# The output projection of a window-attention block: one float32 product becomes three float16 products, with their split on GpSimd

## The reference, cut to what matters

```python
f = _ln(f, g1, b1); f = jnp.roll(f, (-SS, -SS), axis=(1, 2)); win = _window_partition(f)
qkv = win @ w_qkv + b_qkv
attn = softmax(q k^T * scale + mask)
out = einsum('bhij,bhjd->bihd', attn, v).reshape(-1, L, C)
out = out @ w_proj + b_proj                  # the projection that is changed
f = residual + roll_back(window_reverse(out))
m = gelu(_ln(f, g2, b2) @ w_fc1 + b_fc1) @ w_fc2 + b_fc2
return f + m
```

## Time and profile before

| | |
|---|---|
| median of 3 runs | 2864.15 us (2864.08 to 2870.08) |
| the profiled execution | 2863.74 us, its span 2861.9 us |
| busy share of the span | PE 95%, PEld 78%, DVE 85%, ACT 74%, POOL 64% |
| granted TensorE clock | 0.995 of full speed |
| instructions | PE 55491, DVE 6634, ACT 3464, POOL 2344 |

### The profile page before, as it was taken

One profiled execution on the slowest core, in us unless ns is written; L12 is line 12 of the kernel. 1 busy time (PEld: TensorE's weight loads), 2 busy tenths in 40 slices (PEclk: granted clock), 3 DMA queues, 4 the chain that ended last, 5 costly groups with the idle time before them and its releaser, 6 DMA issues.

```text
span 2861.9 us, 138054 instructions
## 1 busy us (share of the span) xinstructions
PE 2724.4 (95%) x55491; PEld 2241.3 (78%) x55491; DVE 2427.8 (85%) x6634; ACT 2113.9 (74%) x3464; POOL 1844.0 (64%) x2344
## 2 busy tenths in 40 slices
PE   4999999999999999999999999999999999999996
PEld 2788787888878878878878888887887887878885
DVE  7888888888888888888888888888888888888884
ACT  2677777777777777777777777777777777777774
POOL 4566666666666666666666666666666666666665
PEclk9999999999999999999999999999999999999998
DMA  3454544545545445454454554544545445455441
GB/s 84 125 131 127 133 128 129 132 124 133 132 124 132 129 128 132 125 133 128 129 134 124 131 132 126 131 129 127 133 126 132 126 130 134 124 131 132 127 118 29
DMA packets 414852, 358.88 MB, mean 125 GB/s; under 512 B 63646, under 2 KB 414176, under 8 KB 414204
## 3 DMA queue, kind: packets, MB, share of 16 engines
q1 hardware_dynamic: 414220, 350.04, 46.7%
HBM read 193.29 MB, written 154.14 MB: 121 GB/s over the span
## 4 chain that ended last, share of the span: by engine, by line
PE 69%; DVE 18%; issue 7%; ACT 5%; POOL 1%; SPq 0%; DMA 0%; POOLq 0%; DVEq 0%
PE psum L530 11%; PE psum L438 9%; PE psum L512 8%; DVE nmax L856 7%; PE psum L570 7%; DVE yr L920 6%; PE psum L618 6%; PE psum L494 6%; ACT probs L719 4%; PE psum L652 4%; PE psum L555 3%; PE psum L448 3%; PE psum L608 3%; PE psum L456 3%; PE psum L658 3%
## 5 line engine op out<-in xcount | busy, mean ns | idle before, releaser
L719 ACT ACTIVATE probs<-psum 113x784 f32<-113x784 f32 x768 | 631.2, 822 | 314.7 <-PE psum L512 311.6
L856 DVE TENSOR_REDUCE nmax<-psum 113x16 f32<-113x784 f32 x768 | 743.1, 968 | 70.3 <-PE psum L494 70.1
L530 PE MATMUL psum<-vbd,probs 128*49 128x18 f32 x24576 | 643.1, 197 | 7.4 <-issue 6.6
L530 PEld LDWEIGHTS psum<-vbd,probs 128*49 128x49 f32 x24576 | 632.5, 126 | 10.7 <-issue 10.5
L399 POOL TENSOR_SCALAR ve<-mv 112x7 f32<-112x7 f32 (+1 forms) x264 | 65.4, 248 | 876.5 <-PE psum L570 638.1
L512 PE MATMUL psum<-qbd,kst 128*49 128x196 f16 x6144 | 405.1, 250 | 36.6 <-issue 16.8
L494 PE MATMUL psum<-kbd,qst 128*49 128x196 f16 x6144 | 402.4, 250 | 27.9 <-DVE nmax L856 25.0
L406 POOL TENSOR_TENSOR rs<-ve,half 112x7 f32<-112x7 f32 (+1 forms) x264 | 394.1, 1493 | 0.0
L411 POOL TENSOR_TENSOR xn<-xn,rs 112x672 f32<-112x672 f32 (+1 forms) x264 | 342.2, 1296 | 73.9 <-POOL rs L406 73.9
L880 DVE BATCH_NORM_STATS2 st<-tok 112x6 f32<-112x96 f32 x1824 | 318.2, 245 | 58.9 <-ACT tok L726 44.8
L392 POOL TENSOR_TENSOR hidl<-hid,hidh 128x588 f16<-128x588 f32 x256 | 333.6, 1303 | 46.2 <-POOL hidh L389 46.2
(11 more groups left out here) (102 smaller groups left out, 6166.7 us busy)
## 6 DMA issues: line engine op xcount, KB each, us to landing
stack_pages<-nat SPq DMA_DIRECT2D x256, 294.0 KB, 3.1
kst<-stack_pages SPq DMA_DIRECT2D x256, 220.5 KB
qbd<-stack_pages SPq DMA_DIRECT2D x1024, 55.1 KB
stack_pages<-nat SPq DMA_DIRECT2D x256, 147.0 KB, 2.0
xr<-in_x_dram SPq DMA_DIRECT2D x224, 147.0 KB, 2.7
out_dram<-yr SPq DMA_DIRECT2D x224, 147.0 KB, 2.1
qst<-stack_pages SPq DMA_DIRECT2D x256, 73.5 KB
kbd<-stack_pages SPq DMA_DIRECT2D x1024, 18.4 KB
```

The lines of the kernel that those rows point to most:

```text
L530: last = nc.tensor.matmul(dst[:, :, h, :], probs[:, b.c % 2, h // 4, p, h % 4 * L:(h % 4 + 1) * L], vbd[:, b.c % 4, p * NH + h, :, :], sta ...
L719: nc.scalar.activation(probs[0:PR, b.c % 2, u, :, :].rearrange("j (g q) k -> j g (q k)", g=2), wide_bank()[0:PR, LEFT:LEFT + 8 * SPAN].rea ...
L856: nc.vector.tensor_reduce(dst, psum[0:PR, A:A + 2, 0:2 * CH].rearrange("i g (q h j) -> i g q h j", q=2, j=L), axis=AX.X, op=ALU.max, negat ...
```

## The change

The projection becomes three float16 products like the others. Its weights are multiplied by 64 and split once (`split_wp`, DVE); its bias becomes a 97th row of the weights, against a row of ones in `oTh`. POOL gets a new job in every step, `split_out`: a rounding of `oT` to `oTh` and a subtraction into `oTl`, 96 x 392 each. It stands in POOL's queue behind `split_hidden` and ahead of `normalise`. The projection waits for the second of the two (`o_low`) instead of for ACT's copy, and `residual` scales by 1/64.

The order changes too. PE: in even steps `contract` goes ahead of `project`, which is then last; in odd steps `scores` 0 goes ahead of `values`, and `out_transposes` goes from behind the expands to right behind `turn`. ACT: in odd steps `out_by_channel` goes ahead of the two gelus, and a gelu of one element stands right behind the third exp. DVE: in odd steps `residual` goes behind `back_low` and `queries_keys_low`. At the start, one of the 15 constant loads (the bias row) is issued only after DVE has filled the padding rows.

```diff
+            const(wp[C:C + 1, :], bproj.rearrange("(a c) -> a c", a=1))
...
+            def split_out(b):
+                pool.wait_ge(o_in, b.count(2, 2))
+                alone(pool)
+                wait(pool, proj_made, b.count(1))
+                alone(pool)
+                nc.gpsimd.tensor_copy(oTh[0:C, :], oT[:, :]).then_inc(o_high, 1)
+                pool.wait_ge(o_high, b.count(1, 1))
+                alone(pool)
+                nc.gpsimd.tensor_tensor(oTl[0:C, :], oT[:, :], oTh[0:C, :], ALU.subtract).then_inc(o_low, 1)
...
                             split_hidden(t.step(offset))
+                if has(t.step(WEIGH)):
+                    split_out(t.step(WEIGH))
...
-                pe.wait_ge(o_in, b.count(2, 2))
+                pe.wait_ge(o_low, b.count(1, 1))
...
-                nc.tensor.matmul(psum[0:C, V_BANK, 0:TOK], wp[:, :], oT[:, :], start=True, stop=True).then_inc(proj_made, 1)
+                for n, (weights, rows) in enumerate(((wph, oTh), (wph, oTl), (wpl, oTh))):
+                    last = nc.tensor.matmul(psum[0:C, V_BANK, 0:TOK], weights[:, :], rows[:, :], start=n == 0, stop=n == 2)
+                last.then_inc(proj_made, 1)
...
                     shifted(t, 0)
+                    scores(t, 0)
                     values(t)
-                    scores(t, 0)
...
                     turn(t)
+                    out_transposes(t)
                     expand(t, 0)
...
                     max_transpose(t)
-                    out_transposes(t)
                     back(t)
...
                     queries_keys(t)
+                    contract(t)
                     project(t)
-                    contract(t)
...
+            nc.vector.memset(spare[:, :], 0.0).then_inc(filled, 1)
             dve.wait_ge(filled, 1)
+            nc.vector.memset(oTh[C:C + 1, :], 1.0)
...
+            def split_wp():
+                nc.vector.tensor_scalar(wp[:, :], wp[:, :], GAIN, None, ALU.mult).then_inc(wp_split, 1)
+                dve.wait_ge(wp_split, 1)
+                nc.vector.tensor_copy(wph[:, :], wp[:, :]).then_inc(wp_split, 1)
+                dve.wait_ge(wp_split, 2)
+                nc.vector.tensor_tensor(wpl[:, :], wp[:, :], wph[:, :], ALU.subtract).then_inc(wp_split, 1)
...
+            def gelu_table(t):
+                nc.scalar.activation(spare[0:1, 1:2], spare[0:1, 0:1], ACT.Gelu)
...
                     run(PROB, exps, 2)
+                    run(HIDDEN[0], gelu_table)
+                    run(WEIGH, out_by_channel)
                     run(HIDDEN[0], gelu, 0)
                     run(HIDDEN[1], gelu, 1)
-                    run(WEIGH, out_by_channel)
...
                 before = t.step(-1)
-                run(before, WEIGH, residual)
                 if odd(t):
                     if turns(before.step(BACK)):
                         back_low(before)
                     run(before, QK, queries_keys_low)
+                run(before, WEIGH, residual)
+                if odd(t):
                     run(t, STORE[0], result, 0)
```

More of the change, by code:

```diff
@@ L119, in build @@
         wp, w2 = sb("wp", [FULL, C]), sb("w2", [FULL, 3, C])
-        vec = sb("vec", [C, 6])
-        G1, B1, BP, G2, B2, BF = range(6)
+        vec = sb("vec", [C, 5])
+        G1, B1, G2, B2, BF = range(5)
         xr = sb("xr", [C, 4, WS, SIDE])
@@ L139, in build @@
         on = sb("on", [PR, 2, 2, C])
-        oT = sb("oT", [FULL, TOK])
+        oT = sb("oT", [C, TOK])
+        spare = sb("spare", [1, 2])
+        oTh, oTl = sb("oTh", [FULL, TOK], F16), sb("oTl", [FULL, TOK], F16)
+        wph, wpl = sb("wph", [FULL, C], F16), sb("wpl", [FULL, C], F16)
         hid = sb("hid", [FULL, 2, 3, PART])
@@ L182, in build @@
         ot_made, o_in, proj_made, f_made = sem("ot_made"), sem("o_in"), sem("proj_made"), sem("f_made")
-        w2_split = sem("w2_split")
+        w2_split, wp_split = sem("w2_split"), sem("wp_split")
+        o_high, o_low = sem("o_high"), sem("o_low")
         hid_high, hid_low, w2_wide, y_scaled = sem("hid_high"), sem("hid_low"), sem("w2_wide"), sem("y_scaled")
@@ L264, in _ @@
             const(brow1[C:C + 1, :], bfc1.rearrange("(a c) -> a c", a=1))
-            for n, v in ((G1, g1), (B1, b1), (BP, bproj), (G2, g2), (B2, b2), (BF, bfc2)):
+            for n, v in ((G1, g1), (B1, b1), (G2, g2), (B2, b2), (BF, bfc2)):
                 column(n, v)
             sp.wait_ge(filled, 1)
+            const(wp[C:C + 1, :], bproj.rearrange("(a c) -> a c", a=1))
             sp.dma_start(xfh[C:C + 1, :, :, :].rearrange("a n k t -> a (n k) t"), rows_d[0, 4:5, 0:8, :]).then_inc(rows_one, 16)
@@ L614, in project @@
                     return
-                pe.wait_ge(o_in, b.count(2, 2))
+                pe.wait_ge(o_low, b.count(1, 1))
                 if has(t.step(SCORE)):
                     pe.wait_ge(max_row, t.step(SCORE).count(1, 1))
-                nc.tensor.matmul(psum[0:C, V_BANK, 0:TOK], wp[:, :], oT[:, :], start=True, stop=True).then_inc(proj_made, 1)
+                if first(b, 0):
+                    pe.wait_ge(wp_split, 3)
+                for n, (weights, rows) in enumerate(((wph, oTh), (wph, oTl), (wpl, oTh))):
+                    last = nc.tensor.matmul(psum[0:C, V_BANK, 0:TOK], weights[:, :], rows[:, :], start=n == 0, stop=n == 2)
+                last.then_inc(proj_made, 1)
             def expand(t, n):
@@ L708, in value_blocks @@
                 if first(b, 0):
+                    act.wait_ge(filled, 1)
                     act.wait_ge(vbd_ones, 1)
@@ L751, in out_by_channel @@
                 act.wait_ge(ot_made, b.count(1, 1))
+                wait(act, o_low, b.count(1))
                 for d in range(2):
@@ L811, in _ @@
             nc.vector.memset(w2[0:REST, 2, :], 0.0)
-            for a in (wide, wide1, wp, xfh, xfl, oT):
-                last = nc.vector.memset(a[FILL:FULL], 0.0)
-            last.then_inc(filled, 1)
+            for a in (wide, wide1, wp, xfh, xfl, oTh, oTl):
+                nc.vector.memset(a[FILL:FULL], 0.0)
+            nc.vector.memset(spare[:, :], 0.0).then_inc(filled, 1)
             dve.wait_ge(filled, 1)
+            nc.vector.memset(oTh[C:C + 1, :], 1.0)
             dve.wait_ge(consts_in, 16 * N_CONST)
@@ L904, in residual @@
                 wait(dve, y_made, b.count(1, -7))
-                nc.vector.scalar_tensor_tensor(out=xf[:, b.c % 8, 1, :], in0=psum[0:C, V_BANK, 0:TOK], scalar=vec[:, BP:BP + 1], in1=xf[:, b.c % 8, 0, :],
-                                               op0=ALU.add, op1=ALU.add).then_inc(f_made, 1)
+                nc.vector.scalar_tensor_tensor(out=xf[:, b.c % 8, 1, :], in0=psum[0:C, V_BANK, 0:TOK], scalar=1 / GAIN, in1=xf[:, b.c % 8, 0, :],
+                                               op0=ALU.mult, op1=ALU.add).then_inc(f_made, 1)
             def result(t, n):
@@ L954, in step @@
                     split_w2()
+                    split_wp()
             steps(dve, step)
```

## The result

The changed kernel takes 2839.14 us (median of 4 runs, 2836.45 to 2842.35) beside 2865.34 us for the kernel before in the same session. The ratio is 0.9906, with a 95% interval of 0.9889 to 0.9923: faster by 0.9%. The forecast was 2931 us, slower by 2.3%, with a range down to 2850; the time lies outside that range and on the other side of no change. The profiled execution of the changed kernel took 2836.45 us, its span 2834.7.

What follows compares the result with a forecast made beforehand. The bound was taken to be a DVE and POOL loop of 21.57 us a pair. 2863.7 + 63 (POOL's overrun delaying result 1) + 3 (start) + about 1 (tail) = 2931 us; likeliest case 2921 to 2955, 8-in-10 range down to 2850.

Steps and rivals of the forecast that it cites:

- the 0.84 us of room: POOL's idle time per pair ahead of the even normalise; split_out's 1.5 us was to overrun it by 0.60 to 0.69.
- The projection's saving on PE: Three float16 products for one float32: 0.17 us a step, 0.33 a pair, costed at nothing.
- The odd step: split_out waits for oT ahead of the odd normalise, done at about 1437.4 where normalise is due at 1437.84: costs nothing.
- the 0.4 us that were to spare: Margin between split_out's end and normalise in the odd step; any delay beyond it would cost one to one.
- who is held at the power: DVE's result 0 waits for POOL's mean subtraction; result 1's first addition then precedes POOL's multiplication by 0.15 to 0.24 us.
- The hold on result 1: DVE's two small additions wait for POOL's 1.31 us multiplication; result 1 over 2 us, the pair 0.45 to 0.69 longer.
- The term that was put at nothing: The float16 products on PE, outside the DVE and POOL loop: nothing, or 42 us if PE set the time alone.
- The other moves: Reordered out_transposes, values, contract and ACT work shift inside gaps that the longer DVE loop widens: nothing.
- The other terms: The start: bias row issued late and landing at about 12.8, so PE begins later: +3 us, once.
- The faster rival: DVE keeps the port between result 1's additions, PE becomes the bound and gains 0.33 us a pair: 2817 to 2835, chance 0.15.
- The table drain: 1.38 us added on ACT to every table load, odd normalise some 0.5 us late; part of slower rival, 2960 to 2995, chance 0.06.

Runs made afterwards that it cites:

- no_read: Kernel before, POOL's even-step multiplication replaced by two memsets that read nothing (a probe only, norms left unfinished): 2821.28 us, ratio 0.9849.
- after_f32: Changed kernel with the projection as one float32 product again, split_out kept and waited for: 2925.84 us, ratio 1.0218.
- half_low: Changed kernel with split_out's subtraction in even steps covering only the first half of the tokens: 2872.01 us, ratio 1.0028.
- f32_later: Changed kernel with one float32 projection product, plus a POOL fill of 96 x 512 behind the even split_out: 2882.64 us, ratio 1.0065.
- after_later: Changed kernel plus a small POOL fill of 96 x 180 behind the even split_out: 2842.45 us, ratio 0.9928.
- pool_long: Kernel before plus one POOL fill of unused memory, 96 x 2240, ahead of the even normalise: 2834.82 us, ratio 0.9898.
- after_rf: Changed kernel with DVE's result 1 moved right behind result 0, ahead of the first maxima: 2849.21 us, ratio 0.9952.
- after_early: Changed kernel with wp's padding filled first under its own semaphore, so the bias row loads with the other constants: 2834.88 us, ratio 0.99.

## Why the prediction was wrong

**What held.** `split_out` takes 0.51 and 0.93 us with 0.18 between, as worked out; the 0.84 us of room are used up. The projection's saving on PE is 0.36 us a pair in the new order (0.33 forecast). The odd step costs nothing: normalise starts 3.04 us behind the end of the third maxima (1419.97 to 1423.01), where it was 2.99 us; but the 0.4 us that were to spare are gone, since `split_out` ends there at 1423.04. POOL and DVE take turns, and result 1 is what it is about: no_read shows it.

**The step that failed: who is held at the power.** "Result 0 is held until the subtraction of the mean is done ... So its first addition comes 0.15 to 0.24 us ahead of the multiplication, and holds it up until about 1430.75." The gap between result 1's start and the multiplication is 0.63 us in the changed kernel. Count from the start of the subtraction of the mean: the multiplication was due 3.05 us later and came 3.33 us later (1413.14 to 1416.47), because the power took 1.78 us instead of 1.51. Result 1 was due 2.81 to 2.90 us later and came after 2.70 (1415.84). Some 0.28 and 0.15 us make 0.63 out of 0.2.

I had let the turn-taking hold only DVE at the power, since result 0 ran beside it for 0.70 us in the earlier trace rows. But there the power had begun 0.69 us ahead of result 0. My own numbers put result 0 at 1428.81 and the end of the subtraction, with which the power starts, at 1428.76 to 1428.85: in the very order that I did not ask about. The hold on result 1 behind that point was sized rightly: after_f32 and half_low have a gap of 0.16 to 0.22 us and a result 1 of 2.15 us (2.25 forecast).

**The term that was put at nothing.** The products were costed at nothing because PE was not in the loop of the kernel before. What they are worth while result 1 is held, no run tells apart (half_low has less POOL work as well). With result 1 free, the float32 product costs 40 us (f32_later against after_later), near the 42 that I had worked out for the case in which PE sets the time alone. The steps from the forecast to the result can be followed in three kernels: after_f32 (2925.84 us, result 1 held, float32 product) is near the forecast of 2931; f32_later (2882.64) has result 1 free; the changed kernel (2839.14) has the float16 products too. So the first step alone takes the forecast to f32_later, which is still slower than the kernel before and within the stated range; it is the second that takes it to a gain. The other moves, also put at nothing, leave PE idle for 0.34 us a pair.

**The other terms.** PE starts 1.89 us later (11.80 instead of 9.91), not 3: the bias row lands 1.20 us behind its issue, where I took 2.13. The last constant's issue and PE's first work in the changed kernel:

```profile
10.60 0.23 SPq L254 DMA_DIRECT2D wp<-in_L_conv_b_proj_dram  x1
...
11.80 1.12 PE L450 MATMUL psum<-wraw,vec 96*1 96x288 f32 x2 [11.80 <-DMA wp<-in_L_conv_b_proj_dram]
```

**The rivals.** The faster rival named the right condition, "as soon as all three are read before the multiplication is ready", and a time of 2817 to 2835 us; the kernel took 2839. Its first half came about by another road: DVE does not keep the port (in after_f32 the multiplication gets in behind the first addition, and result 1 takes 2.15 us), POOL comes late. Its second half, that PE then gains its 0.33 us a pair, is what f32_later shows; but it charged the order edits nothing, where PE pays 0.34 us of idle time. The table drain of the Trainium skill (ScalarE: Activation LUTs, What ACT_TABLE_LOAD costs) is not there. Rows 7 leave out the line behind the odd load of the kernel before: there the gelu comes 0.99 us behind the load, and waits for PE, so these rows could not settle it. On ACT, in the changed kernel, the load starts 0.02 us behind the third exp, and the one-element gelu 0.01 us behind the end of the load:

```profile
1418.39 0.82 ACT L741 ACTIVATE probs<-psum 113x784 f32<-113x784 f32 x1 [0.94 <-PE psum L529]
1419.23 1.28 ACT L781 ACT_TABLE_LOAD   x1
1420.52 0.20 ACT L781 ACTIVATE spare<-spare 1x1 f32<-1x1 f32 x1
1420.63 0.52 ACT L776 ACTIVATE oT<-psum 96x196 f32<-96x196 f32 x2
```

**What stays open.** What sets the new pair. Its median is 21.17 us; pool_long, with the old order and product, has 21.20, and no_read, without `split_out`, 21.18. The chain now passes through PE, POOL and issue, and after_later, after_rf and after_early move it by no more than 0.15 us. I have not taken that loop apart; it is no longer result 1, and by f32_later PE's work is in it.

## What to carry to other kernels

Where two engines take turns at a port, sum the arrival of *both* at *each* instruction of both, the short ones too, and look for places where your forecast puts two arrivals within a few tenths of a microsecond: there the forecast is two forecasts, and the range has to hold both. Before rebuilding a product, put an idle fill of two lengths ahead of the suspect: here that alone gave the whole gain. A saving off the critical path is not worth nothing: here 0.36 us a pair on PE changed who came first (43 us), and once that was settled PE was on the path and the saving was paid as well (40 us).

## What the runs showed of the hardware

I take all pairs of before, of the changed kernel and of the other tabled kernels but no_read, ten in all, with the power and the multiplication at their full size. Where the power started 0.06 to 0.88 us behind result 0, it took 1.77 to 1.82 us, 615 times of 615. Where it started 0.05 to 0.91 us ahead, it took 1.50 to 1.52, 595 of 595, and result 0 took 0.69 to 0.71; between the two both happen. Where the multiplication started 0.55 to 1.0 us behind result 1, result 1 took 0.68 to 0.70 us, 594 of 594; from 0 to 0.45 us behind, 1.80 to 2.19, 252 of 252. The border is sharp: at 0.45 to 0.49 us result 1 took 1.81 to 1.84 (11 pairs), at 0.50 to 0.52 it took 0.69 to 0.70 (10 pairs). So the first addition has done with the port 0.50 us after its start, which is its own time, and the power, once begun, does not hold it.

The Trainium skill (SBUF — State Buffer, Who interferes with whom) gives the exclusion, and the multiplication and the first addition agree with it. The power does not fit the lock for a whole instruction: result 0 takes 0.69 us while a power of 1.51 us runs. The table in the same section of the Trainium skill says that GpSimd's read goes through the shared port, and the 1.78 us show the side that is easily left out: an instruction of POOL that reads seven elements per partition waits too.

The hold on the power is 0.27 us however far ahead result 0 started, while result 0 itself grows with that lead (0.80 us at 0.19, 0.98 at 0.38). Both fit one reading, that result 0 waits for the end of the subtraction's reading and the power then waits for result 0; no run takes it apart further.
